# The second close of a two-layer transformer kernel: first products as three fp32r products of parts made by GpSimd, and the clamp on GpSimd

## The reference

```python
gated = attn @ w_gate + b_gate            # 256 -> 512
a, g = jnp.split(gated, 2, axis=-1)
x = x + a * jax.nn.sigmoid(g)
y = _layernorm(x) / input_scale
x_q = jnp.clip(y, -448.0, 448.0)
x_dq = x_q.astype(jnp.float8_e4m3fn).astype(x.dtype) * input_scale
w_dq = weight_fp8 * weight_scale
x = x + jnp.einsum('bsi,oi->bso', x_dq, w_dq) + bias
```

## Time and profile before

| | |
|---|---|
| median of 3 runs | 2159.44 us (2157.16 to 2160.05) |
| the profiled execution's own time | 2158.82 us |
| its span, first to last instruction | 2157.1 us |
| busy: PE / DVE / ACT / POOL | 91% / 55% / 64% / 37% |
| granted TensorE clock, mean | 0.95 |
| the second close | from about 2050 us to the end |

### The profile page before, as it was taken

How to read it: one execution, slowest core, us unless ns; L and a number is a source line. 1 busy time by engine, 2 the same in 40 slices (tenths; PEclk the granted TensorE clock), 3 DMA queues, 4 the chain that set the end, 5 groups by cost and what they waited for, 6 DMA issues and landing times. The chain is left out here.

```text
span 2157.1 us, 37876 instructions
## 1 busy us (share of the span) xinstructions
PE 1965.9 (91%) x12227; PEld 1132.6 (53%) x12227; DVE 1179.3 (55%) x2115; ACT 1384.8 (64%) x1585; POOL 804.5 (37%) x706
## 2 busy tenths in 40 slices
PE   6989999999956599999999999958899999999897
PEld 5722333323232488888888888857622222222255
DVE  5511163534557723323333333337599999999967
ACT  5689999999933233233233233226599999999943
POOL 2001010111120241443342444211078888988922
PEclk9989999999965699999999999979899999999999
DMA  6753243442210530202202220238944425463011
GB/s 207 232 97 69 46 102 59 107 71 60 59 41 0 195 128 29 87 29 83 91 28 85 89 84 26 86 115 300 300 67 106 94 53 117 59 151 63 27 63 70
DMA packets 76964, 203.63 MB, mean 94 GB/s; under 512 B 13092, under 2 KB 28262, under 8 KB 74664
## 3 DMA queue, kind: packets, MB, share of 16 engines
q1 hardware_dynamic: 67048, 179.26, 31.0%
q0 software_dynamic: 6816, 18.62, 2.5%
q10 hardware_dynamic: 2896, 3.16, 0.5%
HBM read 338.84 MB, written 60.03 MB: 185 GB/s over the span
## 5 line engine op out<-in xcount | busy, mean ns | idle before, releaser
L1291 PE MATMUL psum<-A_qa,A_ka 50*128 50x512 f32 x2048 | 417.7, 473 | 26.6 <-DVE A_qa L1375 7.3
L1291 PEld LDWEIGHTS psum<-A_qa,A_ka 50*128 50x128 f32 x2048 | 177.5, 186 | 476.9 <-DVE A1f_probs L1385 243.3
L2475 PE MATMUL psum<-e_w_high,e_xT 128*128 x1136 | 386.9, 402 | 3.9 <-DVE e_xT L2425 3.8
L1509 POOL TENSOR_TENSOR A1f_probs<-A1f_probs,A1f_bias 128x512 f32<-128x512 f32 x256 | 327.3, 1290 | 83.0 <-ACT A1f_probs L1343 82.6
L1331 ACT ACTIVATE A0f_probs<-psum 128x1024 f32<-128x1024 f32 x256 | 337.1, 1317 | 8.6 <-PE psum L1291 5.4
L1343 ACT ACTIVATE A0f_probs<-psum 128x1024 f32<-128x1024 f32 x256 | 338.5, 1322 | 0.0
L1385 DVE SCALAR_TENSOR_TENSOR A1f_probs<-psum,A1f_bias 128x1024 f32<-128x1024 f32 x256 | 311.7, 1218 | 24.0 <-PE psum L1291 20.7
L2432 DVE TENSOR_TENSOR e_hT<-psum,e_hT 128x1024 fp32r<-128x1024 f32 x71 | 87.0, 1225 | 421.3 <-ACT e_hT L2396 421.3
L1310 PE MATMUL psum<-A1f_probs,v 128*32 128x512 f32 x2048 | 274.4, 607 | 17.3 <-POOL A1f_probs L1509 15.8
L1335 ACT ACTIVATE A1f_probs<-A1f_probs 128x1024 f32<-128x1024 f32 x256 | 273.9, 1070 | 4.7 <-DVE A1f_probs L1385 3.8
L1310 PE MATMUL psum<-A0f_probs,v 128*32 128x512 f32 x2048 | 273.6, 606 | 0.0
(11 more groups left out here) (291 smaller groups left out, 2746.6 us busy)
## 6 DMA issues: line engine op xcount, KB each, us to landing
e_w_raw<-in_experts SPq DMA_DIRECT2D x73, 3072.0 KB, 11.5
qk_parts<-L_part SPq DMA_DIRECT2D x64, 512.0 KB, 3.9
A_qa<-qk_parts SPq DMA_DIRECT2D x192, 128.0 KB, 4.1
A_ka<-qk_parts SPq DMA_DIRECT2D x192, 128.0 KB, 6.1
om<-results SPq DMA_DIRECT2D x16, 512.0 KB, 8.6
A1f_bias<-tables SPq DMA_DIRECT2D x16, 384.0 KB, 8.5
A1f_bias<-tables SPq DMA_DIRECT2D x16, 320.0 KB, 10.4
L_x<-in_x SPq DMA_DIRECT2D x8, 512.0 KB, 6.6
```

What stands on the lines that cost most here:

```text
L1291: mm = e.matmul(ps[:, side * HALF:(side + 1) * HALF], self.qk.ka[rows, s, pair, kt * P:(kt + 1) * P].bitcast(FP32R), self.qk.qa[rows, s, p ...
L1509: e.tensor_tensor(fourth, fourth, self.bias_of(*w[1:], slice(self.FOURTH, GH)).rearrange("p h q -> p (h q)"), ALU.mult).then_inc(self.mult ...
L2475: mm = e.matmul(out, left[part].bitcast(FP32R), moving.bitcast(FP32R), start=start and i == 0, stop=stop and i == 2)
```

## The change

From unit 2 on, each fp32 product of the gate jobs becomes three fp32r products: high part of `omT` by high part of `wg`, high by low, low by high. GpSimd makes the parts: those of `wg` and of unit 2 at the start of the stage (after the last attention product and the last turn), those of unit u + 3 right after it has clamped unit u. Each part is a cast and a subtraction over 128x1024 elements; three buffers hold a unit's parts. The clamp of the normalised tokens moves from VectorE to GpSimd for units 0 to 6; VectorE keeps that of unit 7. Two semaphores are now shared with the first close, whose counts are added to the waits.

```diff
@@ SecondClose.gate_pe
+        if u >= self.PARTED and i == 0:
+            e.wait_ge(self.parted, self.parted_before + u - self.PARTED + 2)
...
-            for k in range(DC):
-                mm = e.matmul(out, self.omT[:, k, at:at + P], self.wg[:, k, :], start=False,
-                              stop=(k == DC - 1))
+            products = list(self.products(u, slice((2 * i + j) * P, (2 * i + j + 1) * P)))
+            for n, (om, w) in enumerate(products):
+                mm = e.matmul(out, om, w, start=False, stop=(n == len(products) - 1))
...
+    def products(self, u, tile):
+        for k in range(DC):
+            if u < self.PARTED:
+                yield self.omT[:, k, u * self.W:(u + 1) * self.W][:, tile], self.wg[:, k, :]
+            else:
+                s = u % self.PART_BUFS
+                for om, w in ((self.om_high, self.wg_high), (self.om_high, self.wg_low), (self.om_low, self.wg_high)):
+                    yield om[:, s, k, tile].bitcast(FP32R), w[:, k, :].bitcast(FP32R)
@@ exponents_dve
-        e.wait_ge(self.normed, u + 1)
-        a = steps.of(e.tensor_scalar(y, y, FP8_MAX, -FP8_MAX, ALU.min, ALU.max))
-        e.wait_ge(steps.sem, a)
+        if u < self.UNITS - 1:
+            e.wait_ge(self.clamped, u + 1)
+        else:
+            e.wait_ge(self.normed, u + 1)
+            a = steps.of(e.tensor_scalar(y, y, FP8_MAX, -FP8_MAX, ALU.min, ALU.max))
+            e.wait_ge(steps.sem, a)
@@ pool
         self.m.pool.of(e.memset(self.power[:, :], -0.5))
+        self.wait_weights(e)
+        e.wait_ge(self.turned, 4 * B)
+        self.part(e, self.wg_high[:, :, :], self.wg_low[:, :, :], self.wg[:, :, :])
+        self.part_pool(e, self.PARTED)
         for u in range(self.UNITS):
             self.root_pool(e, u)
+            if u < self.UNITS - 1:
+                self.clamp_pool(e, u)
+            if u + self.PARTED + 1 < self.UNITS:
+                self.part_pool(e, u + self.PARTED + 1)
+
+    def part(self, e, high, low, whole):
+        steps = self.m.pool
+        a = steps.of(e.tensor_copy(high.bitcast(FP32R), whole))
+        e.wait_ge(steps.sem, a)
+        e.tensor_tensor(low.bitcast(FP32R), whole, high, ALU.subtract).then_inc(self.parted, 1)
+
+    def part_pool(self, e, u):
+        s = u % self.PART_BUFS
+        if u >= self.PARTED + self.PART_BUFS:
+            e.wait_ge(self.gate_full, 2 * (u - self.PART_BUFS + 1))
+        self.part(e, self.om_high[:, s, :, :], self.om_low[:, s, :, :], self.omT[:, :, u * self.W:(u + 1) * self.W])
+
+    def clamp_pool(self, e, u):
+        y = self.xn[:, u % self.BEHIND, :, :]
+        e.wait_ge(self.normed, u + 1)
+        e.tensor_scalar(y, y, FP8_MAX, -FP8_MAX, ALU.min, ALU.max).then_inc(self.clamped, 1)
@@ Program.gpsimd
                 if layer:
+                    self.fast[1].wait_products_done(e)
                     self.second_close.pool(e)
```

More of the change, by code:

```diff
@@ L672 @@
     BY_PE = LAST - 1
+    WEIGHTS = 4
     SINGLES = 3 * DC
@@ L682, in __init__ @@
         self.t = t
-        self.w_in, self.x_in, self.x_biased = sem("c_w_in"), [sem(f"c_x_in{i}") for i in range(2)], sem("c_x_biased")
+        self.w_in, self.x_in, self.x_biased = m.w_in, [sem(f"c_x_in{i}") for i in range(2)], sem("c_x_biased")
         self.turned, self.wo_full, self.wo_out = sem("c_turned"), sem("c_wo_full"), sem("c_wo_out")
-        self.parted = sem("c_parted")
+        self.parted = m.parted
         self.measured, self.rooted, self.normed = sem("c_measured"), sem("c_rooted"), sem("c_normed")
@@ L712, in parts, with parted_before @@
         return [("part", 2 * b + half, c) for c in range(DC) for half in range(2)]
+    def parted_before(self):
+        return 1 + sum(len(self.parts(b)) for b in range(B))
     def heavy(self, u):
@@ L749, in wait_weights @@
     def wait_weights(self, e):
-        e.wait_ge(self.w_in, 4 * DMA)
+        e.wait_ge(self.w_in, self.WEIGHTS * DMA)
     def wait_stored(self, e):
@@ L1260, in wait_scores_read, with wait_products_done @@
         e.wait_ge(self.exped[1], n)
+    def wait_products_done(self, e):
+        e.wait_ge(self.pv_done, len(self.order) * 2 * BT)
     def wait_scored(self, e):
@@ L2545 @@
     BEHIND = 3
+    PARTED, PART_BUFS = 2, 3
     LOW_ROW = 32
@@ L2551, with __init__ @@
     STEP, LEAST = 1.5 * 2.0 ** 20, 2.0 ** -6
-    def __init__(self, m, omT, t, x2_dram, out_dram):
+    def __init__(self, m, omT, t, x2_dram, out_dram, close):
         sem = m.sem
         self.m, self.t = m, t
+        self.loaded_before, self.parted_before = close.WEIGHTS, close.parted_before()
         self.omT = omT.rearrange("p n d -> p (n d)").rearrange("p (c n) -> p c n", c=DC)
@@ L2558, in __init__ @@
         self.out_dst = out_dram.rearrange("(u t p) d -> u p t d", p=P, t=self.TILES)
-        self.w_in, self.x_in, self.out_done = sem("f_w_in"), [sem(f"f_x_in{i}") for i in range(3)], sem("f_out")
+        self.w_in, self.parted, self.clamped = m.w_in, m.parted, sem("f_clamped")
+        self.x_in, self.out_done = [sem(f"f_x_in{i}") for i in range(3)], sem("f_out")
         self.split = sem("f_split")
@@ L2599, in allocate @@
         self.x = sb("f_x", [P, self.UNITS, T, D])
+        self.wg_high, self.wg_low = (sb(f"f_wg_{name}", [P, DC, 2 * D]) for name in ("high", "low"))
+        self.om_high, self.om_low = (sb(f"f_om_{name}", [P, self.PART_BUFS, DC, W]) for name in ("high", "low"))
     def load_weights(self, e):
@@ L2610, in wait_weights @@
     def wait_weights(self, e):
-        e.wait_ge(self.w_in, 7 * DMA)
+        e.wait_ge(self.w_in, (self.loaded_before + 7) * DMA)
     def clear_bias(self, e):
@@ L2678, in gate_pe @@
         self.ring.wait_empty(e, job)
+        if u >= self.PARTED and i == 0:
+            e.wait_ge(self.parted, self.parted_before + u - self.PARTED + 2)
         e.wait_ge(self.turned, 2 * B + u + 1 if u == 0 or (u, i) == (1, 0) else 4 * B)
         for j in range(2):
-            out, at = ps[:, j * HALF:(j + 1) * HALF], u * self.W + (2 * i + j) * P
+            out = ps[:, j * HALF:(j + 1) * HALF]
             e.matmul(out, self.m.ones[:, :].bitcast(FP32R), self.bias[:, 0:2 * D].bitcast(FP32R), start=True,
                      stop=False)
-            for k in range(DC):
-                mm = e.matmul(out, self.omT[:, k, at:at + P], self.wg[:, k, :], start=False,
-                              stop=(k == DC - 1))
+            products = list(self.products(u, slice((2 * i + j) * P, (2 * i + j + 1) * P)))
+            for n, (om, w) in enumerate(products):
+                mm = e.matmul(out, om, w, start=False, stop=(n == len(products) - 1))
         mm.then_inc(self.gate_full, 1)
+    def products(self, u, tile):
[6 more added lines that the diff above has]
+                    yield om[:, s, k, tile].bitcast(FP32R), w[:, k, :].bitcast(FP32R)
     def product_pe(self, e, job):
@@ L2867, in __init__ @@
         self.branch_pool = m.sem("branch_pool")
+        m.w_in, m.parted = m.sem("weights_in"), m.sem("parted")
         m.shifted = [m.sem(f"shifted{i}") for i in range(len(Attention.SHIFTED))]
@@ L2934, in __init__ @@
         sb.close()
-        self.second_close = SecondClose(m, om, t, x2_dram, out_dram)
+        self.second_close = SecondClose(m, om, t, x2_dram, out_dram, self.close)
         self.second_close.allocate_weights(second)
```

## The result

The changed kernel takes 2174.78 us (median of 4 runs, 2173.32 to 2175.45) against 2159.74 us for the kernel before (2157.16 to 2161.89, 4 runs): a ratio of 1.0069, 95% interval 1.0055 to 1.0082. It is slower by 15 us. Its profiled execution took 2174.2 us, span 2172.4, 15.3 more than the span before.

What follows compares the result with a forecast made beforehand. The prediction took the second close's loop over VectorE, GpSimd and ScalarE as the bound, not TensorE: five units at 2.76 (13.8 us) plus two clamps at 0.50 (1.0) gave +14.8, 2174.2 us; range 2163.5 to 2177.5.

Steps and rivals of the forecast that it cites:

- The order at the port: Behind clamps 0 to 4, GpSimd's cast gets the shared SBUF port before VectorE's exponent bits; likeliest case, chance 0.55, +14.8 us.
- The held operations: VectorE, units 0 to 4: cast holds exponent bits, +0.82 us; subtraction holds the second residual add, +1.44 us per unit.
- The clamp: Moved to GpSimd but still in the loop: 1.15 us taken, +0.50 us a unit for units 0 to 6.
- A term that the sum put at nothing: TensorE may drop to 1.2 GHz when idle; its lead would cover this, so no time was added.
- That its saving is worth nothing: First products, units 2 to 7: TensorE spared 6.7 us, but it was 2.5 us early, so gain 0.
- TensorE's busy time in the stage down by 6 to 7 us: Second close: sign expected in the new profile, with more TensorE idle, whatever the span does.
- That the bits go first: Rival at the port: VectorE's exponent bits precede GpSimd's cast; +4.9 us, 2164.3 us, chance 0.2.
- the late root: If the bits go first, subtraction delays GpSimd's root about 0.5 us; charged only in the first two loops.
- That TensorE sets the pace: Faster rival, first products of units 2 to 7: -6.7 us, 2152.7 us, chance 0.04.
- no exclusion: Rival: VectorE never waits for a long GpSimd operation, only the clamp's cost remains; +3.5 us, 2162.9 us, chance 0.05.

Runs made afterwards that it cites:

- e7: Changed kernel plus a 0.20 us GpSimd memset between the clamp and the cast of units 3 to 7: 2166.44 us, ratio 1.0034; stage 108.80.
- e6: Kernel before, with VectorE's first gate product of unit u+1 moved ahead of the rounding of unit u-1: 2162.57 us, ratio 1.0013; stage 105.16.
- e5: Changed kernel with memsets of about the same length replacing the parts of units 3 to 7; output not the reference's: 2166.49 us, ratio 1.0028; stage 109.27.
- e2: Kernel before with only the clamp moved to GpSimd; no parts, fp32 products throughout: 2163.97 us, ratio 1.0019; stage 105.63.
- e1: Changed kernel, but GpSimd's cast for unit u+3 waits until VectorE has taken unit u's exponent bits: 2168.12 us, ratio 1.0043; stage 109.16.
- e3: Kernel before with the parts and fp32r products, VectorE keeping every clamp: 2166.11 us, ratio 1.0032; stage 108.96.
- e4: Kernel before with fp32r products all from unit 2's parts, later parts left out, clamps on VectorE; output not the reference's: 2161.05 us, ratio 1.0011; stage 102.65.
- e9: e8 plus fp32r products all from unit 2's parts, parts of units 3 to 7 left out; against the kernel before: 2155.36 us, ratio 0.9965; stage 100.24.
- e8: e6 plus a wait: rounding of unit u starts only when unit u+1's root is done; against the kernel before: 2157.88 us, ratio 0.9983; stage 98.77.

## Why the prediction was right

**The order at the port.** The step that carried the forecast was that the cast, 0.05 us before the clamp's end, has the port before the bits. It did in each of the five units (cast 1.04, bits 1.50), and e7 shows that it is the order of issue that decides and not a preference of the hardware: 0.15 us of shift turned it (0.08 before, 0.07 after). The Trainium skill's rule (SBUF — State Buffer, Who interferes with whom), the first to issue holds the pair for the whole instruction, is thus borne out at gaps of 0.07 and 0.08 us, and in e6 of 0.12. The prediction said that no row showed so close a race, but its own do: there L798, at 271.62, came 0.08 before L888, and L888 was held.

One row of the kernel before limits that rule:

```profile
2113.85 1.04 POOL L2838 TENSOR_TENSOR f_rs<-f_rs,f_power 128x4 f32<-128x4 f32 x1
2114.28 1.22 DVE L2811 SCALAR_TENSOR_TENSOR f_xn<-f_step,f_xn 128x1024 f32<-128x1024 f32 x1
```

L2838 raises four elements to a power and has 0.61 us to go when the rounding starts, but the rounding takes its usual 1.22 and isn't held. So this operation doesn't have the port for its whole length. The other way round, behind a rounding, it does wait (2.11 in e7).

**The held operations.** Forecast were +0.82 for the bits and +1.44 for the add, 2.26 per unit. The bits showed 1.50 (+0.81), the add 2.12 to 2.18 (+1.43 to +1.49). Loops with a part grew by 2.64 to 2.71; less the clamp's 0.40 that leaves 2.24 to 2.31. That the bits are excluded I had from their rate, 1024 elements in 0.69, and from L894's 1.14 in the earlier trace rows, not from a row of the bits themselves; the 1.50 shows it, and e5 that their exclusion is another one than the add's.

**The clamp** was mis-sized: 1.15 taken, 1.04 measured, which is my lower bound. +0.40 a loop instead of +0.50, 0.7 us over seven. Its place in the loop was right (e2).

**A term that the sum put at nothing** made up for it: the tail, +0.87. I had said that TensorE might drop to 1.2 GHz and that its lead would cover that. In the loop this holds. TensorE's first records at 1.2 GHz follow 4.83 us of idle:

```profile
2085.74 0.58 PE L2725 MATMUL psum<-f_bias,ones 128*128 128x256 f32 x1 [4.83 <-ACT f_xqT L2780]
```

Two windows of one loop each, the first with a granted clock of 0.87, the second of 1.00:

```profile
2092.00:2105.00 13.00, 10.77 (x52) 8.53 (x50) 9.89 (x15) 5.26 (x9) 7.94 (x8) 0.87 0.12 40
2105.00:2118.00 13.00, 10.46 (x56) 8.45 (x56) 10.82 (x18) 5.27 (x10) 7.94 (x8) 1.00 0.12 42
```

Both loops take 12.84 us. After unit 7's rows there is no lead, and output products and transposes are on the path. In the kernel before the clock came back within the products of unit 6 (granted 1.00 from 2147 to 2151 us), and the eight transposes behind them take 0.89 us in its chain. After the change it did not (0.79 from 2161 to 2165). First before, then after:

```profile
2147.16 0.89 PE psum L2671 x8
...
2161.74 1.40 PE psum L2688 x8
2163.16 1.03 ACT f_xqT L2780
```

From the start of unit 6's products to that of unit 7's it is 7.13 us (2157.10 to 2164.23) against 6.28 before: 0.85, which is nearly all of the tail's 0.87. But that the longer tail belongs to the change isn't shown. e1 and e3, with the same products and parts, have tails of 15.61 and 15.50, shorter than before the change. In single profiles of the eleven kernels the tail lies between 15.50 and 17.36, and the granted clock is low over different parts of it. With e1's tail the stage would be 14.0 us longer than before. So that the sum came out to 0.2 us is luck, two errors that nearly cancel, -0.7 for the clamp and +0.87 for the tail; the blocked operations, 11.4 of the 15 us where 11.3 were forecast, were right.

**TensorE.** That its saving is worth nothing was right (e4), and I read the pitch well: 0.23 to 0.24 where 0.24 was forecast.

```profile
2131.19 0.39 PE L2706 MATMUL psum<-f_wg_high,f_om_high 128*128 128x512 f32 x1
2131.43 0.40 PE L2706 MATMUL psum<-f_wg_low,f_om_high 128*128 128x512 f32 x1
...
2132.58 0.39 PE L2702 MATMUL psum<-f_bias,ones 128*128 128x512 f32 x1
2132.81 0.39 PE L2706 MATMUL psum<-f_wg_high,f_om_high 128*128 128x512 f32 x1
```

From tile to tile it is 1.62 us, bias product included, where it was 1.95 (2119.41 to 2121.36): 0.33 per tile and 7.9 over 24 tiles, where I had 0.28 and 6.7. But "TensorE's busy time in the stage down by 6 to 7 us", and that it "will fall, whatever the span does", was wrong: from the stage's first gate record to its last add it is 93.5 us against 91.8. The forecast mistook busy time for work. In e4, whose stage has the old length, it did fall, to 86.4. Products of the fp8 layer take 40.4 us by their groups where they took 34.7, since more of them run at 1.2 GHz, and a record of 0.39 at a pitch of 0.23 adds its tail wherever a row of products ends. Here the spared TensorE did its next work more slowly.

**The rivals.** That the bits go first is what e1 and e7 made on purpose: 6.4 and 6.0 us of the stage against the rival's 4.9. The direction holds, the price was low. I had the late root cost units 2 to 4 nothing, since it ends with the rounding in any case; but their loops are longer than e2's by 0.72 in e1 and 0.52 in e7, which is about what the add is held (0.33 and 0.12) and the root starts late (0.43). That TensorE sets the pace fell with e4, no exclusion with the bits' 1.50.

**What stays open.** What sets the place of the low clock in the tail, and so the tail's length, is open: the longer tails after the change and in e9 are read from rows and windows of one profile each, and no run held the clock and left the rest.

## What to carry to other kernels

Price an operation moved to GpSimd by what it reads and what VectorE wants at that moment, not by GpSimd's free time: 8 us of work in a loop of 10 fitted, and cost 15 us, two fifths of it from the combination of two moves that alone cost 9. Where two engines share a port, write the order down with a wait; an order that hangs on 0.08 us is worth 9 us either way, and a root of 4 elements let through before a 1.2 us rounding bought more than sparing TensorE 8 us did. Ask of an engine off the path only whether it is waited for, and then look at the end of the stage, where its lead is gone.

## What I had not expected of the hardware

- An operation on four elements, 1.04 us elsewhere, takes 2.11 when it comes 0.02 us behind a rounding on VectorE (e7), but doesn't hold a rounding that comes 0.43 us behind it (1.22, in the kernel before).
- A memset on GpSimd, which reads nothing, holds VectorE's bit mask (1.41 for 0.69) and lets a two-input add through (0.69 inside 2.23).
- 0.12 and 0.22 us of lateness cost the root some 0.9 us each time in e6 (L2848 1.27, L2850 1.06; 0.30 and 0.20 in e8), and with the wait that e8 adds the stage is 4.0 us shorter than before in place of 2.4 longer.
- The tail of the stage, with the same output products, took from 15.50 (e3) to 17.36 us (e9) in single profiles, with the granted clock of TensorE low over different parts of it.
